# Two up-down filters and an attention block on one core: rows of maxima copied by ACT's transfers, a finer second group norm, the second half's bias on VectorE, and new orders on four engines

## The chip, the core and the metric

One core of a Trainium2 chip runs the whole program. The time is the device time of one execution in microseconds. Engines: PE is TensorE, ACT is ScalarE, DVE is VectorE, POOL is GpSimd; SP is used for issuing transfers only. Each engine works through its own list in order and meets the others through semaphores.

## What is computed

The input x has 8 images of 128 channels and 16 x 16 points. First a filtered leaky ReLU: add a bias per channel, upsample by 2 in both directions with a 12-tap filter, leaky ReLU, downsample by 2 with the same filter. Then, on the result y:

```python
x_norm = group_norm(y, gn1_gamma, gn1_beta, 32)
q, k, v = split(qkv_w @ x_norm + qkv_b)            # 8 heads of 16
attn = softmax(q @ k.T / sqrt(16)) @ v
x_attn = group_norm(out_w @ attn + out_b, gn2_gamma, gn2_beta, 32)
h1, gate = split(x_attn.T @ mlp1_w.T)              # 512 each
out = y + (silu(h1) * gate @ mlp2_w.T).T
```

All tensors are float32.

## The kernel before

The tokens of an image are its 256 points. PE does every filter and every projection; a product marked float32r is one pass, plain float32 costs several.

**Filters.** The input comes as six overlapping windows of rows (`win`), each in two quarters of two images (`in_xw`) and one half of four images (`in_xh`), by 18 transfers that SP issues first. The bias is added in place: for the quarters by DVE (`add_bias`, L1499), for the second half by POOL (`add_bias(t)`, L364, one add of 128x512 per window). `upsample(n)` (L790, n = 0 to 15) multiplies windows with a Kronecker weight into one of four PSUM banks, which `leaky(n)` (ACT, L507) reads out; so `upsample(n)` waits for `leaky(n - 4)`. `downsample(b)` (L822) makes image b, and `read_y(b)` (ACT, L515 and L517) copies it and sums its values and squares.

**First group norm.** `group_means(n)` (PE, L806) averages over groups for one batch of images, `variance(n)` (DVE) follows, `first_coefficients(n)` (POOL, L378 to L381) gives scale and shift. `normalise_first` (DVE) normalises image 0, `normalise(i)` (POOL) the others, each split into a high and a low part.

**Attention, image by image.** `project_qk(i)` and `project_v(i)` go into the bank `px`. `high_parts(i)` (ACT, L524) and `low_parts(i)` (DVE, L1531) write the two parts of q and k to `qk_parts`, and six transfers of SP (`stack(i)`, L311) lay them out as `q_stack` and `k_stack` of 128 rows in one of three slots; `fill` (ACT, L500, 128x2048, six in all) clears the slots once. `maxima(i, h, c)` (L862) is half of the scores of head h in bank `pm[h % 2]`, `reduce_max(i, h)` (DVE, L1548) takes the negative row maximum, and after eight heads `turn_maxima(i)` (PE, L876) turns them into a row layout, which `read_rows(i)` (ACT, L578) copies to `max_row`. The transfer `rows(i)` (SP, L317, 8 KB) puts them into the last row of `q_stack`, so that `scores(i, h, c)` (L888) come out with the maximum subtracted, in bank `ps[h % 2]`. `exponentials(i, h)` (ACT, L531) reads that bank; `scores` of head h waits for the exponential of head h - 2. `weigh(i, half, c)` (L913) multiplies with V and a column of ones. Then for the division: `read_sums` (ACT, L549, L550), `merge` (DVE), `turn_sums` (PE, L924), `invert` (DVE), `spread_inverse` (ACT, L557), `turn_inverse` (PE, L931), `normalise` (DVE, L1575), `project_out` (PE, L936), `read_proj` and `square_attn` (ACT, L566, L572).

**Second group norm and MLP.** `GN2_BATCHES` says for which images one `group_means` and one `second_coefficients` (POOL, seven small steps, L388 to L394) serve. `second_norm(i)` (POOL, L447, L449, L452) writes the high and low part of image i. An image has two pairs p = 2i and 2i + 1. `up_project(p, j, e)` (L772 to L774, three products) makes values (j = 0) and gates (j = 1). For p below 8 ACT's `squash` is a tanh and DVE's `swish_value` and `gate` finish; from p = 8 on `squash` is a Silu, with a table load before the first. `split_high(p)` (ACT, L586) and `split_low(p)` (POOL, L424) split the product for `down_project(p, e)`, up to p = 13; 14 and 15 go in plain float32 (L998). `split_high(p)` waits for `down_project(p - 2)`, `gate(p)` for `split_low(p - 2)`. `residual(i)` (DVE, L1602) adds y, `store(i)` (SP) sends the image out.

**Orders.** For each engine a list is written out by hand at the end of its block; `up_project(14)` and `(15)` belong to image 7. SP's list mixes `stack`, `rows`, `load_w1` and `store`.

Of the kernel before, what the change touches and what calls it, by code (L numbers as in the profile page):

```python
# [31 lines left out]
F32 = mybir.dt.float32  # L32
F32R = mybir.dt.float32r
ALU = mybir.AluOpType
# [41 lines left out]
GN2_BATCHES = [(0, 2), (2, 4), (4, 6), (6, 7), (7, 8)]  # L76
# [4 lines left out]
def build(nc, xw, xh, factors, vecs, wqk, wv, wo, w1, w2,  # L81
          ident, gmat, swap, out):
    ctx = ExitStack()
    with ctx:
# [131 lines left out]
        biased_dve, biased_pool = sem("biased_dve"), sem("biased_pool")  # L216
# [65 lines left out]
        def _(sp):  # L282
# [42 lines left out]
            stack(1)  # L325
            load_w1()
            stack(2)
            rows(0)
            rows(1)
            stack(3)  # L330
            rows(2)
            stack(4)
            rows(3)
            stack(5)
            stack(6)
            rows(4)
            rows(5)
            stack(7)
            rows(6)
            store(0)  # L340
            store(1)
            rows(7)
            for j in range(2, 8):
                store(j)
# [4 lines left out]
        def _(pool):  # L349
# [9 lines left out]

            def add_bias(t):  # L360
                pool.wait_ge(fac_in, 16)
                pool.wait_ge(win_in[t][2], 16)
                x4 = win_at(t, 2, 2).rearrange("p (b c) -> p b c", c=C)
                pool.tensor_tensor(x4, x4, bias_bc[:, None, :].to_broadcast([128, B // 2, C]), ALU.add).then_inc(biased_pool, 1)  # L364
# [90 lines left out]
            for j in range(0, 5):  # L455
                add_bias(j)
# [3 lines left out]
            add_bias(5)  # L460
# [9 lines left out]
            second_norm(0)  # L470
            second_norm(1)
            split_low(0)
            second_coefficients(4)
            second_norm(2)
            second_norm(3)
            for j in range(1, 4):
                split_low(j)
            second_coefficients(5)
            second_norm(4)
            split_low(4)  # L480
            split_low(5)
            second_norm(5)
            split_low(6)
            second_coefficients(6)
# [10 lines left out]
        def _(act):  # L495
# [118 lines left out]
            for j in range(7, 10):  # L614
                leaky(j)
# [1194 lines left out]
```

## Time and profile before

| what | us |
|---|---|
| median of 3 runs | 147.03 (146.26 to 147.64) |
| the profiled execution's own time | 146.93 |
| its span, from the first to the last instruction | 145.1 |
| PE busy / ACT busy / DVE busy / POOL busy | 138.5 / 104.5 / 88.2 / 75.2 |

The profiled execution lies 1.8 us around its span and 0.1 from the median. Busy times are sums over an engine's instructions; matmul ends are modelled. "Idle before, releaser" is the time in which the engine stood still before an instruction, and what released it.

### The profile page before, as it was taken

The page shows a single profiled execution, that of the slowest core. Times are in us where ns is not written, and L with a number is a line of the kernel's source. Part 1 is how long each engine was busy: PE and PEld are TensorE (multiplying, and loading weights), DVE is VectorE, ACT ScalarE, POOL GpSimd, SP SyncE. Part 2 cuts the span into 40 slices and gives each one's busy share as a digit, 9 for nine tenths or more (in the row PEclk, how much of TensorE's full clock was granted, in tenths as well). Part 3 has the DMA queues.
Part 4 walks back from the last instruction along what each step waited for, and adds up shares of the span by engine and source line. Part 5 has one row for each costly group of instructions (what it writes and reads, how often), then busy time and mean ns, then how long its engine had stood idle before and what let it go on. Part 6 is the DMA issues. An engine that isn't in the chain of part 4 may idle for free.

```text
span 145.1 us, 3307 instructions
## 1 busy us (share of the span) xinstructions
PE 138.5 (95%) x1150; PEld 122.2 (84%) x1150; DVE 88.2 (61%) x187; ACT 104.5 (72%) x235; POOL 75.2 (52%) x126
## 2 busy tenths in 40 slices
PE   6999888999999999999999999999999999999992
PEld 5899578999988687788896998797997997999891
DVE  1940133077649679699699889768684715634251
ACT  6956997955448688697793996894995995766330
POOL 7008985066584850402840304892108988589930
PEclk9999999999999999999999999999999999999999
DMA  3999200746530061331606103501001010011012
GB/s 110 285 272 338 91 0 15 205 113 185 178 113 0 10 169 49 106 113 42 182 0 175 53 0 85 138 0 38 0 7 38 0 43 0 0 41 36 0 36 72
DMA packets 12368, 12.12 MB, mean 83 GB/s; under 512 B 1600, under 2 KB 11328, under 8 KB 12352
## 3 DMA queue, kind: packets, MB, share of 16 engines
q1 hardware_dynamic: 12208, 11.81, 27.4%
q8 instruction: 9, 0.15, 0.4%
q10 hardware_dynamic: 144, 0.10, 0.2%
q14 instruction: 7, 0.06, 0.1%
HBM read 4.50 MB, written 1.05 MB: 38 GB/s over the span
## 4 chain that ended last, share of the span: by engine, by line
PE 63%; SPq 10%; POOL 9%; DMA 7%; issue 4%; DVE 3%; POOLq 1%; ACT 1%; ACTq 0%
PE ps L888 10%; PE po L913 10%; PE pm L862 9%; SPq L311 6%; SPq L286 4%; DMA win<-in_xh 4%; PE pf L772 3%; PE pf L774 3%; PE pf L773 3%; PE px L772 3%; POOL gated_lo L424 3%; PE po L936 3%; PE px L774 2%; PE px L773 2%; POOL win L364 2%
## 5 line engine op out<-in xcount | busy, mean ns | idle before, releaser
L1548 DVE TENSOR_REDUCE neg_max<-pm 128x2 f32<-128x512 f32 x64 | 42.3, 683 | 11.8 <-PE pm L862 11.2
L531 ACT ACTIVATE up_t<-ps 128x512 f32<-128x512 f32 x64 | 36.0, 595 | 4.6 <-PE ps L888 2.5
L888 PE MATMUL ps<-q_stack,k_stack 128*128 128x256 f32 x128 | 27.6, 302 | 0.0
L862 PE MATMUL pm<-k_stack,q_stack 127*128 127x256 f32 x128 | 26.3, 300 | 0.3 <-DVE neg_max L1548 0.2
L424 POOL TENSOR_TENSOR gated_lo<-win,gated_hi 128x512 fp32r<-128x512 f32 x14 | 18.1, 1304 | 12.6 <-ACT gated_hi L586 12.6
L888 PEld LDWEIGHTS ps<-q_stack,k_stack 128*128 128x128 f32 x128 | 19.5, 189 | 2.3 <-ACT up_t L531 1.0
L862 PEld LDWEIGHTS pm<-k_stack,q_stack 127*128 127x128 f32 x128 | 19.1, 189 | 2.5 <-DVE neg_max L1548 1.0
L913 PE MATMUL po<-up_t,v_aug 128*32 128x256 f32 x256 | 15.7, 382 | 0.0
L772 PE MATMUL pf<-xm_hi,w_hi 128*128 128x256 f32 x44 | 13.4, 304 | 0.3 <-issue 0.3
L586 ACT ACTIVATE gated_hi<-win 128x512 fp32r<-128x512 f32 x14 | 8.8, 631 | 6.6 <-DVE win L1597 4.4
L773 PE MATMUL pf<-xm_lo,w_hi 128*128 128x256 f32 x44 | 12.3, 280 | 0.0
L774 PE MATMUL pf<-xm_hi,w_lo 128*128 128x256 f32 x44 | 12.3, 279 | 0.0
L388 POOL TENSOR_TENSOR sq<-gs 128x2 f32<-128x2 f32 (+1 forms) x5 | 1.0, 195 | 21.2 <-DVE gs L1505 21.2
L913 PEld LDWEIGHTS po<-up_t,v_aug 128*32 128x32 f32 x256 | 7.6, 109 | 5.0 <-issue 0.2
L364 POOL TENSOR_TENSOR win<-win,fac 128x512 f32<-128x512 f32 x6 | 7.5, 1275 | 8.3 <-DMA win<-in_xh 8.3
L772 PEld LDWEIGHTS pf<-xm_hi,w_hi 128*128 128x128 f32 x44 | 8.3, 189 | 1.3 <-issue 1.3
L790 PE MATMUL pf<-win,up_w 128*128 128x256 f32 x32 | 8.1, 386 | 0.9 <-ACT up_t L507 0.9
L1531 DVE SCALAR_TENSOR_TENSOR qk_parts<-px,vec,qk_parts 128x256 fp32r<-128x256 f32 x16 | 6.9, 470 | 2.9 <-ACT qk_parts L525 2.9
L549 ACT ACTIVATE early<-po,vec 128x256 f32<-128x256 f32 x8 | 3.8, 474 | 6.6 <-PE po L913 6.6
L773 PEld LDWEIGHTS pf<-xm_lo,w_hi 128*128 128x128 f32 x44 | 8.3, 189 | 0.0
L790 PE MATMUL ps<-win,up_w 128*128 128x256 f32 x32 | 8.3, 400 | 0.0
L774 PEld LDWEIGHTS pf<-xm_hi,w_lo 128*128 128x128 f32 x44 | 8.3, 188 | 0.0
(149 smaller groups left out, 344.6 us busy)
## 6 DMA issues: line engine op xcount, KB each, us to landing
q_stack<-qk_parts SPq DMA_DIRECT2D x24, 128.0 KB, 2.4
k_stack<-qk_parts SPq DMA_DIRECT2D x24, 128.0 KB, 2.4
win<-in_xw SPq DMA_DIRECT2D x12, 128.0 KB, 3.2
win<-in_xh SPq DMA_DIRECT2D x6, 256.0 KB, 5.5
out<-win SPq DMA_DIRECT2D x8, 128.0 KB, 1.7
win<-in_w SPq DMA_DIRECT2D x1, 512.0 KB, 3.7
w_s<-in_w SPq DMA_DIRECT2D x1, 256.0 KB, 3.6
wqk_s<-in_wqk SPq DMA_DIRECT2D x1, 128.0 KB, 4.1
```

The source lines that it names most:

```text
L364: pool.tensor_tensor(x4, x4, bias_bc[:, None, :].to_broadcast([128, B // 2, C]), ALU.add).then_inc(biased_pool, 1)
L424: pool.tensor_tensor(gated_lo[:, r, :], gated[:, r, :], gated_hi[:, r, :].bitcast(F32), ALU.subtract).then_inc(gated_split, 1)
L531: act.activation(probs[:, h // HALF, h % HALF, :, :].rearrange("p c n -> p (c n)"), ps[:, h % 2, :], ACT.Exp, scale=D ** -0.5).then_inc(pr ...
L586: act.activation(gated_hi[:, r, :], gated[:, r, :], ACT.Copy).then_inc(gated_hi_ready, 1)
L772: pe.matmul(dst, w_hi, x_hi, start=start, stop=False)
L773: pe.matmul(dst, w_hi, x_lo, start=False, stop=False)
L774: return pe.matmul(dst, w_lo, x_hi, start=False, stop=stop)
L790: mm = pe.matmul(up_bank[n % 4][:, j * Q:(j + 1) * Q], up_w[:, UP_WEIGHT_OF[m], :, :].rearrange("p a b -> p (a b)"), win_at(t, q), start=T ...
L862: return pe.matmul(pm[:, h % 2, c * N:(c + 1) * N], stack_rows(q_stack, i, slice(0, TOP))[:, h, c * 128:(c + 1) * 128], stack_rows(k_stack ...
L888: return pe.matmul(ps[:, h % 2, c * N:(c + 1) * N], stack_rows(k_stack, i, slice(0, TOP + 1))[:, h, c * 128:(c + 1) * 128], stack_rows(q_s ...
L913: mm = pe.matmul(po[32 * g:32 * g + 32, 0, half * N:(half + 1) * N], v_aug[:, i % V_RING, c, half, b + 32 * g:b + 32 * g + 32], probs[:, h ...
L1548: dve.tensor_reduce(neg_max[:, i % 2, 2 * h:2 * h + 2], pm[:, h % 2, :].rearrange("p (c n) -> p c n", c=2), AX.X, ALU.max, negate=True).th ...
```

## The change

1. `rows(i)` leaves SP. `read_rows(i)` on ACT now waits for the stack of image i too, copies, waits for its own copy and issues the same transfer itself. SP's list is `stack(0)`, `load_w1`, `stack(1)` to `stack(7)`, then all stores.
2. The second group norm has six batches, with images 0 and 1 apart.
3. POOL's `add_bias` goes. DVE's `add_bias(t, 2)` does it, 128x512 each, after its other adds.
4. New orders on POOL, ACT, PE and DVE. The cut diff shows their two ends; between them MLP steps come earlier: `up_project(0, 0, 0)` now stands in the `scores` of image 2 (before: of image 3), and at the last `weigh` 10 pairs are up-projected and 8 down-projected (before: 8 and 6).

```diff
-GN2_BATCHES = [(0, 2), (2, 4), (4, 6), (6, 7), (7, 8)]
+GN2_BATCHES = [(0, 1), (1, 2), (2, 4), (4, 6), (6, 7), (7, 8)]
...
-            def rows(i):
-
-                sp.wait_ge(rows_read, i + 1)
-                sp.dma_start(stack_rows(q_stack, i, slice(TOP, TOP + 1)).rearrange("o h (c n) -> o (h c) n", c=2).bitcast(F32),
-                             max_row[:, :].bitcast(F32)).then_inc(row_in, 16)
...
             stack(0)
-            stack(1)
             load_w1()
...
+            for j in range(1, 8):
+                stack(j)
+            for j in range(0, 8):
                 store(j)
...
-                pool.tensor_tensor(x4, x4, bias_bc[:, None, :].to_broadcast([128, B // 2, C]), ALU.add).then_inc(biased_pool, 1)
...
+            split_w1()
             split_w2()
-            split_w1()
...
+            second_coefficients(7)
             second_norm(6)
-            for j in range(7, 10):
+            for j in range(8, 11):
                 split_low(j)
-            second_coefficients(7)
-            split_low(10)
+            second_coefficients(8)
             second_norm(7)
             for j in range(11, 14):
                 split_low(j)
...
             def read_rows(i):
+
+                act.wait_ge(stack_in[i % SLOTS], 32 * STACKED * (i // SLOTS + 1))
                 act.wait_ge(turn_done, i + 1)
                 if i:
                     act.wait_ge(row_in, 16 * i)
                 act.activation(max_row[:, :], pm[0:2 * HEADS, 1, 0:128], ACT.Copy).then_inc(rows_read, 1)
+                act.wait_ge(rows_read, i + 1)
+                act.dma_start(stack_rows(q_stack, i, slice(TOP, TOP + 1)).rearrange("o h (c n) -> o (h c) n", c=2).bitcast(F32),
+                              max_row[:, :].bitcast(F32)).then_inc(row_in, 16)
...
             fill(1, 0)
+            for j in range(6, 10):
+                leaky(j)
             fill(1, 1)
-            leaky(6)
+            read_y(2)
             fill(2, 0)
-            for j in range(7, 10):
+            high_parts(0)
+            for j in range(10, 13):
                 leaky(j)
-            read_y(2)
-            high_parts(0)
-            leaky(10)
+            read_y(3)
+            leaky(13)
+            leaky(14)
             fill(2, 1)
-            read_y(3)
+            leaky(15)
             read_early_v(0)
...
             squash(8)
             squash(9)
-            spread_inverse(7)
+            read_sums(7)
             split_high(8)
             split_high(9)
+            squash(10)
+            squash(11)
+            spread_inverse(7)
+            split_high(10)
             read_proj(7)
-            squash(10)
             square_attn(7)
...
             group_means(0)
-            for j in range(8, 11):
+            upsample(8)
+            upsample(9)
+            downsample(2)
+            downsample(3)
+            project_qk(0)
+            for j in range(10, 15):
                 upsample(j)
-            downsample(2)
-            project_qk(0)
-            downsample(3)
-            upsample(11)
             project_v(0)
...
             weigh(7, 1, 1)
...
             up_project(11, 0, 0)
-            down_project(9, 0)
-            down_project(9, 1)
             up_project(11, 0, 1)
+            turn_sums(7)
             up_project(11, 1, 0)
             up_project(11, 1, 1)
             up_project(12, 0, 0)
+            turn_inverse(7)
+            down_project(8, 0)
+            down_project(8, 1)
+            project_out(7)
+            down_project(9, 0)
+            down_project(9, 1)
             up_project(12, 0, 1)
             up_project(12, 1, 0)
+            group_means(8)
             up_project(12, 1, 1)
             up_project(13, 0, 0)
             up_project(13, 0, 1)
+            up_project(13, 1, 0)
+            up_project(13, 1, 1)
             down_project(10, 0)
             down_project(10, 1)
-            up_project(13, 1, 0)
-            up_project(13, 1, 1)
             up_project(14, 0, 0)
             up_project(14, 0, 1)
             up_project(14, 1, 0)
-            up_project(14, 1, 1)
             down_project(11, 0)
             down_project(11, 1)
+            up_project(14, 1, 1)
...
             def add_bias(t, q):
+                n = 1 if q < 2 else 2
                 dve.wait_ge(win_in[t][q], 16)
-                x4 = win_at(t, q).rearrange("p (b c) -> p b c", c=C)
-                dve.tensor_tensor(x4, x4, bias_bc[:, None, :].to_broadcast([128, B // QUARTERS, C]), ALU.add).then_inc(biased_dve, 1)
+                x4 = win_at(t, q, n).rearrange("p (b c) -> p b c", c=C)
+                dve.tensor_tensor(x4, x4, bias_bc[:, None, :].to_broadcast([128, n * B // QUARTERS, C]), ALU.add).then_inc(biased_dve, 1)
...
             variance(0)
             normalise_first()
             low_parts(0)
             variance(1)
+            for j in range(0, 3):
+                reduce_max(0, j)
             low_parts(1)
-            for j in range(0, 6):
+            for j in range(3, 8):
                 reduce_max(0, j)
```

## Rows read from the trace of the kernel before

**Rows 1.** The page, parts 1 and 2: busy us (share) xinstructions; PE's clock by slices

```profile
PE 138.5 (95%) x1150; PEld 122.2 (84%) x1150; DVE 88.2 (61%) x187; ACT 104.5 (72%) x235; POOL 75.2 (52%) x126
...
PEclk9999999999999999999999999999999999999999
```

**Rows 2.** One stretch, first `scores` to last `weigh`: busy us (instructions), clock, DMA

```profile
core 0: us, PE busy (x) PEld busy (x) DVE busy (x) ACT busy (x) POOL busy (x), PEclk, DMA share, GB/s
42.86:119.50 76.64, 75.94 (x698) 65.22 (x698) 59.35 (x119) 61.15 (x147) 35.04 (x65) 1.00 0.21 59
```

**Rows 3.** The chain that ended last: start us, us, what

```profile
75.25 0.43 PE po L936 x2
...
76.50 0.57 PE px L844 x4
...
117.94 0.12 PE pf L772
...
119.62 1.86 PE po L913 x32
...
124.16 0.22 PE po L924 x2
...
129.00 0.30 PE po L806 x2
...
129.63 0.20 POOL sq L388
...
132.04 1.27 POOL gated_lo L424
...
134.48 0.74 POOL xm_lo L452
...
142.58 0.42 DVE win L1602
```

**Rows 4.** Timeline of the start, all engines: start us, us, engine line op tiles [idle <-releaser]

```profile
6.37 3.11 SPq L286 DMA_DIRECT2D win<-in_xh  x6
...
11.49 6.19 POOL L364 TENSOR_TENSOR win<-win,fac 128x512 f32<-128x512 f32 x5 [8.29 <-DMA win<-in_xh]
...
15.77 0.16 DVE L1514 TENSOR_SCALAR gs<-po 128x2 f32<-128x2 f32 x1 [4.59 <-PE po L806]
...
16.04 1.90 ACT L500 ACTIVATE k_stack<-rest 128x2048 fp32r<-128x2048 f32 x1
...
17.64 0.42 POOL L355 TENSOR_SCALAR wqk_hi<-wqk_s 128x256 fp32r<-128x256 f32 x1
...
18.48 1.13 PE L790 MATMUL pf<-win,up_w 128*128 128x256 f32 x4 [0.92 <-ACT up_t L507]
...
22.27 0.36 PE L772 MATMUL px<-xn_hi,wqk_hi 128*128 128x256 f32 x1 [0.83 <-DVE xn_lo L1526]
```

**Rows 5.** Groups of instructions by line: shapes xcount, busy us, mean ns, idle before us

```profile
L1548 DVE TENSOR_REDUCE neg_max<-pm 128x2 f32<-128x512 f32 x64 | 42.3, 683 | 11.8 <-PE pm L862 11.2
...
L1593 DVE TENSOR_TENSOR win<-win,ps 128x512 f32<-128x512 f32 x2 | 1.4, 688 | 3.8 <-POOL gated_lo L424 2.5 <-ACT win L600 1.3
```

**Rows 6.** The tile `max_row`: its transfers, from issue to landing

```profile
DMA to landing us min/median/max: 1.8/1.8/2.2
```

**Rows 7.** Timeline around the first row transfer

```profile
39.84 0.25 ACT L578 ACTIVATE max_row<-pm 16x128 fp32r<-16x128 f32 x1
...
40.56 0.60 SPq L317 DMA_DIRECT2D q_stack<-max_row  x1
```

**Rows 8.** Who waited for whom, all engines: us in total, times, longest us

```profile
PEld pm L862 <- DMA k_stack<-qk_parts: 0.3, 1, 0.3
```

**Rows 9.** Timeline of the end

```profile
122.72 1.28 ACT L600 ACT_TABLE_LOAD   x1
...
124.02 0.60 ACT L600 ACTIVATE win<-pf 128x512 f32<-128x512 f32 x1
...
135.32 0.36 PE L772 MATMUL pf<-xm_hi,w_hi 128*128 128x256 f32 x1 [0.26 <-issue]
```

More of the change, by code:

```diff
@@ L669, in _ @@
-            exponentials(2, 7)
-            read_sums(2)
+            squash(0)
+            high_parts(6)
             exponentials(3, 0)
             exponentials(3, 1)
-            high_parts(6)
+            read_sums(2)
+            split_high(0)
             exponentials(3, 2)
@@ L1095, in _ @@
             maxima(2, 2, 1)
-            project_v(3)
-            weigh(0, 1, 0)
-            weigh(0, 1, 1)
+            project_qk(4)
             maxima(2, 3, 0)
             maxima(2, 3, 1)
+            turn_sums(0)
             maxima(2, 4, 0)
             maxima(2, 4, 1)
+            turn_inverse(0)
+            maxima(2, 5, 0)
+            maxima(2, 5, 1)
             scores(1, 0, 0)
@@ L1126, in _ @@
             turn_maxima(2)
+            group_means(3)
+            project_qk(5)
             scores(1, 6, 0)
-            project_out(0)
             scores(1, 6, 1)
-            project_v(4)
+            scores(1, 7, 0)
             maxima(3, 1, 0)
@@ L1134, in _ @@
             maxima(3, 2, 1)
-            scores(1, 7, 0)
             scores(1, 7, 1)
@@ L1143, in _ @@
             maxima(3, 4, 0)
+            maxima(3, 4, 1)
             scores(2, 0, 0)
@@ L1147, in _ @@
             scores(2, 1, 1)
-            maxima(3, 4, 1)
-            project_qk(5)
-            scores(2, 2, 0)
+            weigh(1, 1, 0)
+            weigh(1, 1, 1)
             maxima(3, 5, 0)
             maxima(3, 5, 1)
-            turn_sums(1)
+            project_v(5)
+            maxima(3, 6, 0)
+            maxima(3, 6, 1)
+            scores(2, 2, 0)
             scores(2, 2, 1)
             scores(2, 3, 0)
-            scores(2, 3, 1)
-            maxima(3, 6, 0)
-            maxima(3, 6, 1)
-            turn_inverse(1)
             maxima(3, 7, 0)
             maxima(3, 7, 1)
+            scores(2, 3, 1)
+            up_project(0, 0, 0)
+            turn_sums(1)
             scores(2, 4, 0)
             scores(2, 4, 1)
+            up_project(0, 0, 1)
             maxima(4, 0, 0)
@@ L1222, in _ @@
             maxima(5, 2, 1)
-            project_v(6)
-            up_project(0, 1, 0)
+            scores(3, 7, 0)
+            scores(3, 7, 1)
+            up_project(1, 1, 1)
+            project_qk(7)
             maxima(5, 3, 0)
+            scores(4, 0, 0)
+            scores(4, 0, 1)
+            scores(4, 1, 0)
+            scores(4, 1, 1)
             maxima(5, 3, 1)
-            up_project(0, 1, 1)
+            maxima(5, 4, 0)
+            maxima(5, 4, 1)
             weigh(3, 0, 0)
@@ L1635, in _ @@
-            for j in range(5, 8):
+            for j in range(3, 7):
                 reduce_max(1, j)
             low_parts(3)
-            for j in range(0, 4):
-                reduce_max(2, j)
+            reduce_max(1, 7)
+            reduce_max(2, 0)
+            reduce_max(2, 1)
             merge(0)
+            reduce_max(2, 2)
+            invert(0)
+            reduce_max(2, 3)
             reduce_max(2, 4)
+            normalise(0)
             reduce_max(2, 5)
-            invert(0)
+            low_parts(4)
```

665 lines of the change are left out of this document (308 added, 357 removed).

## The prediction, made before the changed kernel was run

> **What bounds the kernel now.** I read the page's busy table and clock row first, then sums over stretches, then the timelines of both ends. The reader is to see in the first that TensorE (PE) is busy 95% of the span at the full granted clock, and ACT, the next, 72% [rows 1]. So the time is PE's work plus the places where PE waits. From the first `scores` to the last `weigh` ACT is busy 61.15 us of 76.64, 80% [rows 2].
>
> I count PE's work by the hand-written order, with starts that follow each other in the trace. One 256-column product of the split projections takes 0.12 us, so a step of three 0.36 and a half of a `maxima` or `scores` 0.12. One image's `weigh` takes 1.86 (with a further 0.2 until the next product, 2.06), `project_v` 0.57, `project_out` 0.43, a turn 0.22, a group mean 0.3 with its wait [rows 3]; without it I take 0.22. From the first `scores` (42.86) to the last `weigh` (119.55) the old order has 128 + 105 halves, 32 up and 12 down steps, 5 `project_qk`, 5 `project_v`, 7 of each turn and of `weigh`: 72.4 us of work in 76.7, so 4.3 us of waits. After the last `weigh` (end W = 121.5) come 19.9 us of work in 21.1, then 2.5 us to the end (the last residual starts at 142.58 [rows 3]; store, landing): the span ends at W + 23.6.
>
> Two large holes stand in the start: PE is idle 0.92 us at 18.48, until ACT, held by a `fill` of 1.90, reads a bank, and 0.83 us at 22.27, until POOL has done its biases and image 0 is normalised [rows 4].
>
> **The start.** POOL's six bias adds of some 1.2 (five in 6.19, from 11.49) go; six on DVE cost 0.69 each, the price of a DVE tensor-tensor of the same 128x512 [rows 5], 4.1 us. Their cover is that DVE stands idle 4.59 us before 15.77, and the landings space them: POOL's first add waits for the first until 11.49, the six issues take 3.11 in all [rows 4], so the last lands at 14 to 14.8, and its add ends by 15.5, before the group mean can be read at 15.77. Without that cover `variance(0)` would slip by up to 0.7. POOL can then split wqk at about 15.8 (its data, issued behind the windows, has to land) instead of 17.64; from there to `project_qk(0)` at 22.27 it was 4.6 us through coefficients and `normalise_first` [rows 4], so the operand is there at 20.4. PE meanwhile does upsample 8, 9 and downsample 2, 3, as ACT now reads banks 6 to 9 before the next fill: work without a hole to 20.9. Both holes go: -0.9 - 0.8, and about 0.4 of slow restarts.
>
> What is late next (the steps between: an activation of 512 columns 0.6 [rows 9], one of 256 some 0.4 to 0.5, `low_parts` 0.87, a hop between engines 0.1, estimates from the same timelines): the fills still cost 1.9 each and now stand later. `fill(2,1)` runs 27.1 to 29.0, then `leaky(15)`, then `read_early_v(0)` to 30.0, and `project_qk(1)` waits for that copy: +0.5. Then DVE paces: `reduce_max` of 0.68 [rows 5] with `low_parts(1)` before the fourth, the eighth ends at 38.8, after `read_y(7)`. Row 0 is read at about 39.4; its transfer of 1.8 us from issue to landing [rows 6] issued at 39.8 lands at 41.6, and the fourth `maxima` of image 1 goes then too: +0.4. First `scores` at 41.65 instead of 42.86: **-1.2**. The bounds are 0 (DVE's chain is as late as before) and -2.1 (nothing late next).
>
> **The row transfers.** Eight issues leave SP and go to ACT. Before, row 0 was copied at 39.84 to 40.09 and issued at 40.56, behind the stack transfers, in 0.60 [rows 7]; the 0.5 of queueing goes, and is in the 41.65. Each issue holds ACT 0.6 or a little less (SP's row, the nearest), and some 0.05 for the wait on its own copy; queued behind it are the next exponential and so the next-but-one `scores`, as `ps` has two banks. Seven in the middle: 7 x 0.65 = 4.5 us on ACT, plus 2 squashes of 0.6 and one copy of V that come before the last `weigh`: 61.2 + 6.1 = 67.3 of about 81. I take 0 on the path: ACT's idle 15.4 us shrinks to about 14. The bounds are -0.5 (rows land earlier) and +4.5 (each issue felt by PE in full).
>
> PE waits once for a stack, 0.3 us, for the k rows of image 3 [rows 8]. Its slot comes free with the last `scores` of image 0, which the new order has ahead of the second half of `weigh(0)` and 1.2 earlier, while the `maxima` that need it come later: **-0.3**.
>
> The Trainium skill ("DMA: Bandwidth & Descriptors", section "Issuing engines are not separate DMA queues") says that initiating DMAs from several engines saves only the sequencer's time to initiate. By that rule the landing stays 1.8 and the one gain is the 0.5 us of queueing, as the row of row 0 has it; were it false, and two queues also landed faster, the sum would be lower by some tenths.
>
> **Batches and orders.** Six batches instead of five add a group mean on PE (0.22) and, on POOL, coefficients of 2.4 us (129.63 to 132.04) [rows 3], beside PE's work: cost 0.2, which is in the start's sum already. What they allow: image 0's MLP starts at 53.5 instead of 61.0 us of PE's priced work, and by the last `weigh` 40 up and 16 down steps are done, not 32 and 12: 8 x 0.355 + 4 x 0.355 = 4.26 more. So the middle is 77.1 us of work, **+4.7** (one `project_v` and less by one `maxima` half beside), and the end 15.7, less by 4.3. If all else stood, that would be a shift of work and nothing else. But the end hangs on a chain, not on work.
>
> **The chain behind the last `weigh`.** Before, read off [rows 3, 9]: group mean at W + 7.5 (129.0), the coefficients to 132.04, one `split_low` of 1.27, the norm of image 7 to 134.48 + 0.74 = 135.2, so 1.9; `up_project(14)` at 135.32 after an idle 0.26, then 7.3 us to 142.58. The old order has 5.7 us of PE work between group mean and `up_project(14)`; so it nearly covers POOL.
>
> After: read sums at W + 0.3; they now come behind the table load of 1.28 and two squashes, which PE's 3.1 us from the last `scores` to W cover. Merge to W + 2.1; `turn_sums`, reciprocal to 3.0; ACT spreads it only behind `split_high(8)`, `(9)`, `squash(10)`, `(11)`: to 3.95; `turn_inverse` 4.0; `down(8)`; `normalise` 4.4 to 4.85; `project_out` 4.95 to 5.4; `split_high(10)` waits for `down(8)` and holds `read_proj` until 5.8; square to 6.95; group mean at W + 7.15. POOL: 0.6 + 2.4 + 1.9, norm done at W + 12.0. On PE only `up(12,1,1)`, `up(13)` and `down(10)` lie between, 0.36 + 1.42 + 0.71 = 2.5 us, from W + 7.4 to 9.9: **a hole of 2.2 us**. Then `up(14)` at W + 12.1 and 7.3 us, of which 0.2 is a wait for `split_low(11)`: W + 19.4, and 2.5: the span ends at **W + 21.9**, where work alone would give W + 18.2. Against the 23.6 of before: -1.7, for 4.3 us of work less. The bounds are -3.5 (W + 20.1: ACT's order costs nothing and every step follows at once) and -0.7 (POOL or ACT late by another 1 us).
>
> The Trainium skill ("ScalarE: Activation LUTs", section "What ACT_TABLE_LOAD costs") gives a load about 1283 ns plus a drain of about 1380. The load here starts at 122.72, takes 1.28, and the next activation starts at 124.02 [rows 9]: no drain behind it. By the page the sums would be read some 1.3 us later.
>
> **The sum**, against the profiled run: -1.2 - 0.3 + 4.7 - 1.7 = +1.5, a span of 146.6 instead of 145.1. With the 1.83 us around the span (146.93 less 145.1) **148.4 us**. The median before, 147.03, is 0.1 above that run. About 1% (1.5 us) is what a measurement of this kernel tells from no change.
>
> **The rivals.**
> A, faster: the middle loses its waits. For it: 4.3 us of them are there, 2.3 of them by 61 us, and more MLP steps lie beside attention from image 0 on, to fill them. Against it: most of them come before the first MLP step. If it loses 3.5 of 4.3, 148.4 - 3.2 = 145.2. It decides for a gain of 1% from 2.9 us on.
> B, slower: ACT becomes the bound of the middle. Its place is the pair of `ps` banks: an issue of 0.65 beside a row copy of 0.25 is longer than the 0.6 by which one exponential leads. For it: ACT at 83% in the middle with exponentials, squashes and splits in one queue; with 3 us of the 4.5 felt, 151.4. It decides from 0.1 us on for 1%.
> C, the end is shorter: ACT's and DVE's steps of the chain come 1.8 us sooner, W + 20.1: 146.6. Against it: the POOL steps, 4.9 us, are read off and can't shrink.
> D, the change doesn't do what it says: the holes of the start return elsewhere and the end is work-bound as before: 147.0.
> E, the drain of the table load, a mechanism of the end: ACT's queue stays shut after the load for as long again as the load of 1.28 [rows 9], before the sums: 149.7. Against it: the 0.02 us behind the load of before.
> The page "ScalarE: Activation LUTs" of the Trainium skill is what speaks for E.
>
> **How the numbers follow.** Forecast 0.38, A 0.22, B 0.20, C 0.10, D 0.08, E 0.02. The forecast's own spread of about 1 us puts 0.24 of its 0.38 within 1% (145.5 to 148.5) and 0.14 above. A gives 0.17 faster and 0.05 same; B 0.19 slower, 0.01 same; C 0.03 faster, 0.07 same; D 0.07 same, 0.01 faster; E slower. In sum faster 0.21, same 0.44, slower 0.35. The range leaves out 1 in 10 on either side: 145.0 (rival A's time, less 0.2) and 150.4 (two thirds of B's 3 us felt).
>
> **What would show it.** Right: PE without a hole over 0.3 us from 15.6 to 27; first `scores` at 41.3 to 42.0; last `weigh` starting at 122 to 123.5; PE idle 1.5 to 3 us before `up_project(14)`, released by POOL's norm; end at W + 21 to 22.5; transfers of rows landing 1.7 to 2.3 after an ACT issue of 0.4 to 0.65. Wrong: the last `weigh` before 121.5 (A), after 125 with PE waiting for ACT's exponentials (B), no hole before `up_project(14)` (C or D).

## The result, and the profile after

The kernel after takes 149.4 us (median of 6, 148.34 to 150.25), the kernel before beside it 146.75 (6 runs): a ratio of 1.019, 95% interval 1.015 to 1.023. It is slower by nearly two per cent. The sum had forecast a loss of a little over half that size, and its 148.4 us is 1.0 short; of the three outcomes, no change had the highest chance. Medians are of all runs; ratios leave out slow runs, over 1.5% above the fastest of the same kernel.

The profiled execution took 150.02 us, 148.2 of them the span. Parts 1 and 2 of the page of the kernel after, as in [rows 1]:

```profile
PE 139.7 (94%) x1152; PEld 123.7 (83%) x1152; DVE 91.5 (62%) x194; ACT 104.1 (70%) x235; POOL 69.3 (47%) x127
...
PEclk9999999999999999999999999999999999999599
```

PE has two products more (the sixth batch) and 1.2 us more of busy time, in a span that is 3.1 longer (products at a lower clock count as longer busy, so the difference in work is not read from here); the clock row, all nines before, dips once, near the end. A view of stretches says where the time went (columns as in [rows 2]: us, busy us of each engine, granted clock, DMA share, GB/s; cut at the first `scores`, the start of the last `weigh`, and the hole behind it):

```profile
15.00:20.00 5.00, 4.53 (x32) 4.17 (x32) 2.18 (x8) 4.55 (x6) 3.37 (x8) 1.00 0.17 58
20.00:25.00 5.00, 5.00 (x33) 4.65 (x32) 1.39 (x3) 4.74 (x11) 1.02 (x2) 1.00 0.08 21
...
41.64:123.54 81.90, 80.51 (x739) 69.67 (x737) 61.03 (x123) 62.35 (x149) 36.93 (x72) 1.00 0.23 65
...
132.00:137.16 5.16, 2.92 (x25) 2.74 (x24) 0.85 (x2) 2.07 (x4) 3.97 (x12) 1.00 0.07 25
137.16:148.20 11.04, 8.46 (x50) 7.90 (x50) 3.34 (x6) 1.83 (x3) 3.71 (x3) 0.83 0.10 36
```

The holes of the start [rows 4] are gone: behind the 0.47 us at its edge in which the group mean waits for its matrix, PE is busy without a break from 15.6 to 25. The first `scores` stands at 41.64; from there to the last `weigh` it is 81.9 us instead of 76.7 [rows 2], where the prediction's prices give 4.7 us more of PE work. In the last two rows PE is idle for 2.24 of 5.16 us, and then the granted clock is 0.83 on average.

The first row transfer in the timeline, against [rows 7]: ACT copies, issues at once, and its next instruction names the copy as what it waited for.

```profile
39.15 0.27 ACT L550 ACTIVATE max_row<-pm 16x128 fp32r<-16x128 f32 x1
...
39.45 0.60 ACTq L552 DMA_DIRECT2D q_stack<-max_row  x1
...
40.16 0.26 ACT L513 ACTIVATE out_bias<-po,vec 128x1 f32<-128x1 f32 x1 [0.74 <-ACT max_row L550]
```

The timeline of the end, against [rows 9]. POOL's chain from the group mean's variance to the norm of image 7 is unbroken, and ends at 137.06; `up_project(14)`, which needs that norm, starts at 137.16 after 2.24 us without a product. From 137.7 to 141.1 one product is followed by the next after 0.21 us, not 0.12:

```profile
131.98 0.35 PE L779 MATMUL po<-mv,gmat_s 128*128 128x2 f32 x2
...
132.67 0.19 POOL L361 TENSOR_TENSOR sq<-gs 128x1 f32<-128x1 f32 x1 [0.46 <-DVE gs L1478]
...
134.64 0.28 PE L750 MATMUL px<-gated_hi,w_lo 128*128 128x256 f32 x1
...
136.34 0.72 POOL L425 TENSOR_TENSOR xm_lo<-up_t,xm_hi 128x256 fp32r<-128x256 f32 x1
...
137.16 0.36 PE L748 MATMUL pf<-xm_hi,w_hi 128*128 128x256 f32 x1 [2.24 <-issue]
...
138.16 0.42 PE L748 MATMUL pf<-xm_hi,w_hi 128*128 128x256 f32 x1
...
138.37 0.42 PE L749 MATMUL pf<-xm_lo,w_hi 128*128 128x256 f32 x1
...
138.58 0.42 PE L750 MATMUL pf<-xm_hi,w_lo 128*128 128x256 f32 x1
```

The end in both kernels and in five of the experiments below, read off their timelines (us; "behind" is from the end of the last `weigh` to the end of the span; the work beside it is what PE's order holds behind the last `weigh`, by the prices of the prediction):

| profiled run | last `weigh` ends | last group mean | `up_project(14)` | span ends | behind | PE work behind |
|---|---|---|---|---|---|---|
| before | 121.5 | 129.0 | 135.3 | 145.1 | 23.6 | 19.9 |
| after | 125.5 | 132.0 | 137.2 | 148.2 | 22.7 | 15.7 |
| e3, hole filled | 125.4 | 132.0 | 137.2 | 146.9 | 21.4 | 15.7 |
| e10, new middle and end | 126.4 | 133.0 | 138.2 | 147.8 | 21.4 | 15.7 |
| e2, old end | 123.8 | 131.2 | 137.6 | 147.4 | 23.6 | 19.9 |
| e11, half held | 124.1 | 131.2 | 137.5 | 147.3 | 23.2 | 17.8 |
| e12, six batches | 123.1 | 130.7 | 136.9 | 146.8 | 23.6 | 19.9 |

### The profile page after: what moved, and what is told of

The parts are those of the page before. It is cut to its first block, busy times and chain, and to the rows that moved or that the text cites. A ratio compares the mean times of both kernels' runs of the same rounds, so it can differ in the third digit from the quotient of the medians.

```text
span 148.2 us, 3318 instructions
## 1 busy us (share of the span) xinstructions
PE 139.7 (94%) x1152; PEld 123.7 (83%) x1152; DVE 91.5 (62%) x194; ACT 104.1 (70%) x235; POOL 69.3 (47%) x127
## 4 chain that ended last, share of the span: by engine, by line
PE 80%; SPq 6%; DMA 5%; DVE 3%; issue 3%; ACT 1%; ACTq 0%
PE ps L861 11%; PE po L886 10%; PE pm L835 10%; SPq L286 5%; PE pf L748 4%; PE pf L749 4%; PE pf L750 4%; PE px L748 3%; DMA gmat_s<-in_gmat 3%; PE px L749 3%; PE px L750 3%; PE px L817 3%; PE ps L763 2%; PE pf L763 2%; PE pm L795 2%
## 5 line engine op out<-in xcount | busy, mean ns | idle before, releaser
L501 ACT ACTIVATE up_t<-ps 128x512 f32<-128x512 f32 x64 | 35.2, 599 | 9.2 <-PE ps L861 5.6
L835 PE MATMUL pm<-k_stack,q_stack 127*128 127x256 f32 x128 | 27.7, 306 | 0.6 <-DVE neg_max L1521 0.5
L861 PE MATMUL ps<-q_stack,k_stack 128*128 128x256 f32 x128 | 25.5, 296 | 0.3 <-DMA q_stack<-max_row 0.3
L861 PEld LDWEIGHTS ps<-q_stack,k_stack 128*128 128x128 f32 x128 | 18.8, 189 | 2.4 <-issue 0.8
L749 PE MATMUL pf<-xm_lo,w_hi 128*128 128x256 f32 x44 | 12.8, 290 | 0.0
L1472 DVE TENSOR_TENSOR win<-win,fac 128x256 f32<-128x256 f32 (+1 forms) x18 | 8.9, 513 | 2.5 <-DMA win<-in_xw 2.1
L378 POOL TENSOR_SCALAR win<-y,scale,shift 128x256 f32<-128x256 f32 x7 | 4.0, 576 | 9.0 <-PE px L817 8.7
L748 PE MATMUL px<-gated_hi,w_hi 128*128 128x256 f32 x24 | 7.8, 325 | 0.0
```

The costliest lines, as they stand in the source:

```text
L501: act.activation(probs[:, h // HALF, h % HALF, :, :].rearrange("p c n -> p (c n)"), ps[:, h % 2, :], ACT.Exp, scale=D ** -0.5).then_inc(pr ...
L748: pe.matmul(dst, w_hi, x_hi, start=start, stop=False)
L749: pe.matmul(dst, w_hi, x_lo, start=False, stop=False)
L835: return pe.matmul(pm[:, h % 2, c * N:(c + 1) * N], stack_rows(q_stack, i, slice(0, TOP))[:, h, c * 128:(c + 1) * 128], stack_rows(k_stack ...
L861: return pe.matmul(ps[:, h % 2, c * N:(c + 1) * N], stack_rows(k_stack, i, slice(0, TOP + 1))[:, h, c * 128:(c + 1) * 128], stack_rows(q_s ...
L1472: dve.tensor_tensor(x4, x4, bias_bc[:, None, :].to_broadcast([128, n * B // QUARTERS, C]), ALU.add).then_inc(biased_dve, 1)
```

## The experiments

Twelve kernels ran. The kernel before ran beside each group (medians of 146.6 to 147.2 us); times are medians, ratios are to it.

**Parts alone.** First the start by itself: the second half's bias goes to DVE, and PE's, ACT's and DVE's orders are those of the kernel after up to the first scores, then the rest of the kernel before's.

```
-                    if q < 2:
-                        pe.wait_ge(biased_dve, NWIN * q + t + 1)
-                    else:
-                        pe.wait_ge(biased_pool, t + 1)
+                    pe.wait_ge(biased_dve, NWIN * min(q, 2) + t + 1)
...
             stack(0)
-            stack(1)
             load_w1()
+            stack(1)
             stack(2)
             rows(0)
```

> The kernel before with the new start alone: bias of the second half on DVE, the new orders of all engines up to the first scores, then the old orders; rows by SP, five batches. Theory (the loss of the change comes behind the last weigh, the new start is a gain of 1.2 us of which the attention's first waits may take some back): 1.2 us faster than before, ratio 0.992; at least not slower than 0.998. Rival 1 (the new start is late for DVE and ACT, and its gain is lost at once): ratio 1.000. Rival 2 (the bias on DVE is part of the loss): over 1.005.

152.31 us, ratio 1.041 (1.032 to 1.050): by the number the second rival, but not for its reason. SP's issues and the first `scores` in its timeline:

```profile
38.58 0.27 ACT L578 ACTIVATE max_row<-pm 16x128 fp32r<-16x128 f32 x1
...
43.55 0.61 SPq L311 DMA_DIRECT2D k_stack<-qk_parts  x1
...
44.21 0.60 SPq L317 DMA_DIRECT2D q_stack<-max_row  x1
...
46.17 0.58 PE L898 MATMUL ps<-q_stack,k_stack 128*128 128x256 f32 x1 [2.72 <-DMA q_stack<-max_row]
```

The row was copied at 38.58 and issued at 44.21: `rows(0)` stands behind `stack(2)` on SP, and the new orders make that stack's parts later and the row earlier. So the run shows nothing of the start; it shows that the start needs the row out of the stacks' way, on ACT or ahead of `stack(2)`. The run with that one line moved:

```
             stack(1)
-            stack(2)
             rows(0)
+            stack(2)
```

> As the earlier run with the new start alone on the kernel before (second half's bias on DVE, new orders up to the first scores, rows issued by SP, five batches), with one thing changed: on SP the first row transfer stands ahead of the third stack, not behind it. Left of the whole change: its start. Theory (the 5.6 us lost there were the row waiting behind that stack's issues): row issued at 38.6 to 39.6, first scores at 41.2 to 41.9, accumulation in the middle as in the kernel before, 145.2 to 146.0 us. Rival (the new start itself delays DVE or ACT, and the row only hid it): first scores at 41.2 to 41.9 all the same, but the gain is gone by scores(1,0), 146.5 to 147.5. Second rival (something else than the row held the first scores): first scores after 44, over 150.

147.33 us, ratio 1.004 (1.000 to 1.008). The 5 us came from that place, but not from the wait alone: the profiled spans differ by 3.9 us, 2.7 of them the wait. The rest is the clock behind it: with the wait, the granted clock was 0.50 from 44 to 48 and six products of `project_qk` followed each other after 0.21 us, not 0.12. The time of this run is the first rival's, but the first `scores` came at 43.44, later than either theory has it, because the joined order had left `project_v(2)` ahead of it, where PE waited 0.97 us. With it behind, as in the kernel after:

```
-            project_v(2)
             scores(0, 0, 0)
             scores(0, 0, 1)
+            scores(0, 1, 0)
+            scores(0, 1, 1)
+            maxima(1, 4, 0)
+            maxima(1, 4, 1)
+            project_v(2)
```

> As the run with row 0 first (the kernel before with the new start alone, rows by SP, row 0 ahead of the third stack), with one thing changed: project_v(2) and ACT's copy of its result stand behind the first four scores, as in the kernel after; in both earlier runs of this start they stood ahead of them, and PE waited 0.97 us there for the low parts on DVE and spent 0.43 us on the projection. Left of the whole change: its start. Theory (the whole of what the start lost there is this wait): first scores at 41.4 to 42.0, accumulated work and waits 1.0 to 1.5 us under that run to the end, 145.8 to 146.4 us, a ratio to the kernel before of 0.992 to 0.998. Rival (DVE's or ACT's queue behind the start gives the gain back in the first head pair): first scores at 41.4 to 42.0 and 146.6 to 147.4 us.

147.38 us, ratio 1.005 (1.001 to 1.009), 12 runs. The rival holds. The first `scores` is at 41.49, 1.4 earlier than in the kernel before, and `scores(1, 0, 0)` is at 51.86, where it was at 51.92. PE's waits in the window 40 to 46 of its timeline:

```profile
41.15 0.50 PE L872 MATMUL pm<-k_stack,q_stack 127*128 127x256 f32 x2 [0.55 <-DVE neg_max L1564]
...
42.62 0.68 PE L854 MATMUL px<-wv_s,win 128*128 128x128 f32 x4 [0.26 <-DVE qk_parts L1547]
...
43.87 0.36 PE L785 MATMUL px<-xn_hi,wqk_hi 128*128 128x256 f32 x1 [0.56 <-ACT v_aug L537]
```

The wait at 41.15 is ahead of the first `scores`. Behind it stand 0.26 and 0.56, for DVE's low parts and for ACT's copy of V; a further 0.19 at 45.96 is in the kernel before too. Another 0.57 of the 1.4 was never a gain: it is `project_v(2)`, which stands ahead of the first `scores` in the kernel before and behind it here. `project_qk(3)` starts at 43.87, where it was at 43.94, so the gain has gone 2.4 us after the first `scores`.

The complement, the new middle and end (six batches, the kernel after's orders from the first scores on) behind the old start, rows by SP:

```
-GN2_BATCHES = [(0, 2), (2, 4), (4, 6), (6, 7), (7, 8)]
+GN2_BATCHES = [(0, 1), (1, 2), (2, 4), (4, 6), (6, 7), (7, 8)]
```

> The complement of the run with row 0 first: the kernel before's start (bias on POOL, its orders up to the first scores) and rows by SP in the kernel before's SP order, with six batches and the kernel after's orders from the first scores to the end. First scores at 42.6 to 43.0. If the parts add, it is the kernel after less ACT's issues plus the start's gain given up: 149.4 - 2.2 + 1.1 = 148.3 (147.9 to 148.8). If the new middle and end cost nothing by themselves and only ACT's issues did, 146.7 to 147.3; if they cost all of it and ACT's issues nothing, 150 to 151.

157.72 us, for the first experiment's reason, at another place (and again with the clock at 0.50 behind the wait, from 85 to 91); SP's queue and PE in its timeline:

```profile
77.69 0.25 ACT L587 ACTIVATE max_row<-pm 16x128 fp32r<-16x128 f32 x1
...
83.50 0.60 SPq L317 DMA_DIRECT2D q_stack<-max_row  x1
...
85.48 0.79 PE L910 MATMUL ps<-q_stack,k_stack 128*128 128x256 f32 x2 [4.93 <-DMA q_stack<-max_row]
```

Row 4 stood behind `stack(6)`, which the new orders make later. With `rows(4)` ahead of `stack(6)` and `rows(0)` ahead of `stack(2)`:

> As the earlier run of the new middle and end behind the old start (six batches, orders of the kernel after from the first scores on, rows by SP), with SP's order mended: row 4 stands ahead of the seventh stack, row 0 ahead of the third. In the earlier run row 4 was copied at 77.9 and issued at 83.5, and PE stood idle for 4.9 us before scores(4,0). Theory (that wait and what it pushed is all that was wrong, and the parts add): first scores at 42.6 to 43.3, no idle over 0.5 before scores(4,0), last weigh starts at 124 to 125, 149.4 to 150.4 us, which is the kernel after plus the start's 1.1 with nothing back for ACT's issues. Rival (rows by SP give the 2 us back that ACT's issues cost in the old orders): 147.4 to 148.4 us.

150.03 us, ratio 1.023 (1.018 to 1.028). So the new middle and end cost over 2% by themselves (2.8 us by medians of all runs, some 3.4 by the ratio). With the new start before them the ratio is 1.019; the intervals overlap, but the timelines tell the start's worth. The first `scores` is at 42.88 here and at 41.64 in the kernel after, the first `weigh` at 46.56 and 45.83, the last at 124.52 and 123.54. Of the 1.2 us, 0.57 is again `project_v(2)`, now behind the first `scores`; the other 0.7 arrives and stays. In the old orders nothing of it did. (PE still waited 0.45 us before `scores(4, 0, 0)`, for a row that took 3.0 us to land.)

Six batches alone; the added group mean stands ahead of `weigh(1)`:

> The kernel before with six batches in the second group norm and nothing else: windows 0 and 1 get a batch each; the one more group mean stands ahead of weigh(1), its reading behind reduce_max(3,2), the coefficients of window 0 and its second norm on POOL one batch early; all other steps in the kernel before's order. Theory (the batches are free where they stand, the cost of the change is in the end): one product pair of some 0.2 us more on PE, one more short chain on DVE and POOL, 146.8 to 147.4 us against 146.9, a ratio of 0.999 to 1.004. Rival (the group mean waits on ACT's squares in front of weigh(1) and holds the attention behind it): 0.6 us and more, over 147.5.

148.14 us, ratio 1.008 (1.005 to 1.011). The rival holds. Two lines of PE in its timeline:

```profile
58.96 0.35 PE L815 MATMUL po<-mv,gmat_s 128*128 128x2 f32 x2 [0.36 <-ACT y_squares L581]
...
59.76 0.59 PE L922 MATMUL po<-up_t,v_aug 128*32 128x256 f32 x5 [0.45 <-DVE gs L1520]
```

The first `scores` is 0.1 us earlier than in the kernel before, and the last `weigh` starts 1.6 us later. The products of the group mean take 0.2 us, but PE waits 0.36 for ACT's squares ahead of them and 0.45 behind them, because `weigh` writes the bank from which DVE still has to read the means. That is about 1.0 us, the price at this place; of a wait of 0.42 us for k rows, at 55.9, the kernel before had 0.3 [rows 8]. In the kernel after the group mean stands elsewhere, and its price there was not measured alone.

**Who issues the rows.** The kernel before, with the row transfers alone moved to ACT (`read_rows` waits for the image's stack too, as in the kernel after; ACT never stood idle there in this trace):

```
                 act.activation(max_row[:, :], pm[0:2 * HEADS, 1, 0:128], ACT.Copy).then_inc(rows_read, 1)
+                act.wait_ge(rows_read, i + 1)
+                act.dma_start(stack_rows(q_stack, i, slice(TOP, TOP + 1)).rearrange("o h (c n) -> o (h c) n", c=2).bitcast(F32),
+                              max_row[:, :].bitcast(F32)).then_inc(row_in, 16)
```

> The kernel before with the rows' transfers issued by ACT alone, every order else as before. Theory (an issue of 0.5 to 0.6 on ACT hides in ACT's idle time): within 0.5 us of before, ratio 0.998 to 1.004. Rival B of the prediction (ACT is the bound of the middle): 7 issues felt in half or more, 2 us or more, ratio from 1.014. A second rival: rows that land earlier gain, ratio under 0.998.

149.09 us, ratio 1.017 (1.011 to 1.023): 2.5 us slower. Its profiled span is 1.7 longer, and three waits of PE behind such issues hold 1.06 of it in plain idle time (0.21, 0.60, 0.25); the second and the third of them in its timeline:

```profile
66.49 0.25 ACT L569 ACTIVATE max_row<-pm 16x128 fp32r<-16x128 f32 x1
...
66.77 0.51 ACTq L571 DMA_DIRECT2D q_stack<-max_row  x1
...
67.38 0.42 ACT L562 ACTIVATE y_squares<-up_t 128x256 f32<-128x256 f32 x1 [0.64 <-ACT max_row L569]
...
68.04 0.35 PE L800 MATMUL po<-mv,gmat_s 128*128 128x4 f32 x2 [0.60 <-ACT y_squares L562]
...
87.62 0.53 ACTq L571 DMA_DIRECT2D q_stack<-max_row  x1
...
88.25 0.60 ACT L521 ACTIVATE up_t<-ps 128x512 f32<-128x512 f32 x1 [0.66 <-ACT max_row L569]
...
88.90 0.38 PE L882 MATMUL ps<-q_stack,k_stack 128*128 128x256 f32 x1 [0.25 <-ACT up_t L521]
```

An issue shut ACT's compute for 0.64 to 0.66 us. Where the group mean's squares were queued next, PE waited 0.60 of it; where it was an exponential, 0.25. The other way round, the kernel after with the rows back on SP, each ahead of the stack two further on:

> The kernel after with one thing taken back: SP issues the eight row transfers, each ahead of the stack two further on (rows 0 ahead of stack 2, and so on), and ACT no longer waits for the stack before its copy. Theory A (ACT's issues are what the middle paid for: they cost the kernel before 2.5 us when ACT took them over): PE's accumulated waits at scores(7,7) fall from 5.1 to 2.5 to 3.5 us, last weigh starts at 121.0 to 122.0, 147.0 to 147.8 us. Theory B (the middle pays for its own work and its order, ACT's issues lie beside): the waits stay within 0.5 us and the time at 149.0 to 149.8. First scores stay at 41.3 to 42.0 in both.

149.74 us, ratio 1.017 (1.008 to 1.026): theory B. Beside the 1.019 of the kernel after, ACT's issues cost nothing in the new orders that can be measured. That speaks against theory A (147.0 to 147.8), but with four runs some tenths of a microsecond would not be seen, and SP's own queueing is in the number. (In its profiled execution the last k rows of one stack took 4.2 us to land, and PE waited 0.6 us; in that of the next run they took 2.3.)

**The end.** The kernel after with 17 products that nobody reads in the hole, writing a bank that is free there:

```
+            def keep_busy(n):
+                pe.wait_ge(gn_read, len(GN_BATCHES))
+                for _ in range(n):
+                    pe.matmul(po[:, 0, 0:N], w1_hi[:, 0:C], w1_hi[:, 0:N], start=True, stop=True)
...
             down_project(10, 1)
+            keep_busy(17)
             up_project(14, 0, 0)
```

> The changed kernel with 17 products of 0.12 us in the hole before up_project(14), which write a bank that is overwritten later (they add nothing to the output). Theory of two parts (2.2 us of waiting for POOL, and behind it some 3.4 us at the lower clock, 16 products of 0.21 instead of 0.12): the hole's time stays, the lower clock goes, so 1.0 to 1.5 us less than the changed kernel in runs where that showed the lower clock, ratio to before 1.008 to 1.012. Rival (the lower clock has nothing to do with the hole): the same low stretch and the same time, ratio 1.016 to 1.02.

148.68 us (148.59 to 148.99), ratio 1.014 (1.009 to 1.018), 0.7 below the kernel after by medians. The two intervals overlap (1.015 to 1.023 there), so the size is not well known. The stretches in it that answer to the last two of the kernel after:

```profile
132.00:137.15 5.15, 4.90 (x41) 4.73 (x41) 0.84 (x2) 2.02 (x4) 3.96 (x12) 1.00 0.07 25
137.15:146.90 9.75, 7.12 (x50) 6.45 (x50) 3.27 (x6) 1.83 (x3) 3.72 (x3) 0.97 0.12 40
```

`up_project(14)` starts at the same 137.15, so the filling makes nothing ready sooner; but the granted clock stays at 0.97, and the last stretch takes 9.75 us instead of 11.04.

The clock of the single executions bears on it. Three kernels have the hole (the kernel after, with rows on SP, and the new middle and end on the old start): six of their 14 executions have a mean clock of 0.987 to 0.989, all others at least 0.998. With the hole filled it is none of eight. But the hole is not the only place: four of the ten executions of the kernel with row 0 first show the same 0.987 or 0.988, without a hole in the end, and so does one of 16 of the kernel before. The profiled run there is at 1.0, so no trace shows where. The same filling with the rows on SP:

> As the run before it (kernel after, rows by SP), with 17 products that nobody reads put behind down_project(10), where PE stands idle for 2.2 us in the kernel after; they write a bank that is free there. If the two costs add, it is 0.6 to 0.8 us below the run before it: 146.3 to 147.1 under theory A, 148.3 to 149.1 under theory B. If the hole changes its size because ACT is early, the filling costs what it saves and the two runs are within 0.3 us.

148.78 us, ratio 1.013 (1.007 to 1.019): within 0.1 of the run with the rows on ACT, theory B a second time.

The kernel after with four MLP steps (`up_project` 8 and 9, `down_project` 6 and 7) taken back behind the last `weigh`, in the kernel before's orders there:

> The changed kernel, but the MLP's advance at the last weigh taken back: up_project 8 and 9 and down_project 6 and 7 stand behind it, and from there on the orders of before. Theory: the span ends 23.6 us behind the last weigh, which comes 4.3 us earlier than in the changed kernel (125.4), so a span of 144.7 and a time 3 us below the changed kernel's, ratio to before 0.995 to 1.00; no hole over 0.5 us and no lower clock in the end. Rival (ACT's issues or the fuller middle cost the time, the end only shifts work): the time of the changed kernel within 0.7 us, ratio 1.014 to 1.02.

149.66 us, ratio 1.020 (1.014 to 1.027): the rival's time. The last `weigh` ends 1.7 us earlier, not 4.3. PE waits beside the last scores for what the steps had covered:

```profile
118.17 0.70 PE L927 MATMUL po<-weighted,wo_s 128*128 128x256 f32 x2 [0.52 <-DVE weighted L1573]
...
120.01 0.50 PE L879 MATMUL ps<-q_stack,k_stack 128*128 128x256 f32 x2 [0.68 <-ACT up_t L507]
```

Half of that, only `up_project(9)` and `down_project(7)` held back:

> The kernel after with half of what the run with the old end took back: only up_project(9) and down_project(7) go behind the last weigh (six products' groups of 0.355, 2.1 us of PE), up_project(8) and down_project(6) stay beside the scores of the last head pair; behind the last weigh the kernel before's orders. Theory (the loss is in the end: advanced steps fill ACT-bound waits beside the last scores, but more than is needed there, and then are missing between group mean and up_project(14)): accumulated work and waits at the last scores 141.1 to 142.2, no idle over 0.5 us before up_project(14), granted clock 1.0 there, the end longer than that sum by 3.7 as in the kernel before: span 144.8 to 145.9, 146.6 to 147.7 us. Rival (ACT's work in the last pair is too late whatever PE has beside it, so the waits of 2.2 us that the full taking back showed return in full): last weigh starts at 122.8 to 123.6, 148.3 to 149.3 us.

149.38 us, ratio 1.019 (1.014 to 1.025). Neither theory. The last `weigh` started at 122.02, 1.5 earlier, there was no hole before `up_project(14)` and no low clock. But two waits stood behind the last `weigh`, which had been covered:

```profile
125.02 1.28 ACT L581 ACT_TABLE_LOAD   x1
...
126.13 0.41 PE L915 MATMUL po<-swap_s,dens 128*128 128x128 f32 x2 [0.77 <-DVE merged L1558]
...
126.32 0.60 ACT L581 ACTIVATE win<-pf 128x512 f32<-128x512 f32 x1
...
127.76 0.44 PE L922 MATMUL po<-ident_s,inv_wide 128*128 128x128 f32 x2 [0.52 <-ACT inv_wide L533]
```

With an earlier last `weigh` the sums are still read, merged and inverted at ACT's and DVE's pace. In the table the group mean moves from 132.0 to 131.2 only, and `up_project(14)` is 0.3 us later, not earlier.

Why so little comes back ahead of the last `weigh` is seen in the stretch from the start of `weigh(6)` to that of `weigh(7)` in the four timelines (us; work by the prices of the prediction):

| profiled run | `weigh(6)` | `weigh(7)` | stretch | PE work in it | up and down steps, counted as in the prediction |
|---|---|---|---|---|---|
| before | 109.94 | 119.55 | 9.61 | 9.3 | 8 / 4 |
| after | 112.08 | 123.54 | 11.46 | 11.5 | 12 / 6 |
| e11, half held | 112.05 | 122.02 | 9.97 | 9.3 | 8 / 4 |
| e2, old end | 112.05 | 121.82 | 9.77 | 7.2 | 4 / 2 |

Everything that the two runs took back came from this stretch, and with less work than some 9.7 us in it PE waits for ACT and DVE instead. The kernel after has four more up and two more down steps than the kernel before ahead of `weigh(6)` as well; no run took those back.

No version beat the kernel before.

## Why the prediction was right in its direction, and where it was short

- **The first `scores`:** 41.65 predicted, 41.64 measured, by the path described: no PE hole between the group mean and 25 us, the row copied at 39.15, issued at 39.45 and landed 1.9 us later.
- **That this -1.2 goes into the sum:** it holds in the new orders. The sum took -1.2 at the first `scores` and put one `project_v` more (0.57) into the middle, so some -0.7 net; the kernel after is 0.73 ahead of the run with the old start at the first `weigh`, and 0.98 at the last. In the old orders the same start gave nothing: PE's next waits, 0.26 and 0.56 us, took it back within 2.4 us. The line "Then DVE paces" was read up to the first `scores` and no further; that the new orders have other work at that place was not part of the argument.
- **The middle:** the first term that was too small. Work +4.7 and stack -0.3 were to make the stretch 4.4 us longer; it became 5.2 longer (81.9 against 76.7), with the last `weigh` at 123.54, just past the upper end of 122 to 123.5. The priced work is 77.1, so the waits grew from 4.3 to 4.8 where the sum had them shrink to 4.0. PE's named waits in the stretch are 1.08 us (0.24 for low parts, 0.38 and 0.20 at `turn_sums(0)` and `turn_inverse(0)`, 0.26 for row 4), against 0.39 before: that is 0.7 of the 0.8. Nothing of rival A was seen.
- **ACT's issues:** the value of 0 on the path held in the new orders within the scatter (ratios 1.017 and 1.013 with SP, 1.019 and 1.014 with ACT). Rival B is refuted for this kernel, but in the old orders the same edit costs 2.5 us, near the 3 that B had given it. The issue took 0.51 to 0.61 us; from issue to landing it was 1.8 to 2.8 us, median 2.1, where the sign to look for had been 1.7 to 2.3.
- **The hole:** 2.2 us predicted, 2.24 measured, at the place named and behind the chain named; the group mean was at W + 6.6 instead of W + 7.15, `up_project(14)` at W + 11.7 instead of W + 12.1. That the size fits to 0.04 is luck in part: PE and POOL were both some 0.5 early.
- **The end:** W + 21.9 predicted, W + 22.7 measured in the profiled run. With the hole filled it is W + 21.4, and W + 21.4 too in the run with the new middle and end on the old start, which has a hole of 2.28 us and kept its clock. So the chain was priced 0.5 too long, and 1.3 was missing altogether: the products behind the hole were priced at 0.12 us, and took 0.21. This is the second term that was too small. It does not strike every execution: two of the six of the kernel after show a mean clock of 0.987 and 0.989 (spans 148.2 and 148.4), the other four at least 0.998 (146.5 to 147.9). By medians the filling gave back 0.7.
- **Rivals C, D and E:** C's shorter end is there in part once the clock is kept (21.4, between 21.9 and 20.1), hidden by the clock in the profiled run. D falls: the start's holes did not return. E falls: in the kernel after the load stands at 123.47 for 1.28 us and the next activation at 124.77, in the half-held run at 125.02 and 126.32, 0.02 behind it both times. The trace goes against the drain that the Trainium skill ("ScalarE: Activation LUTs", section "What ACT_TABLE_LOAD costs") adds to a load.

In spans the forecast was 146.6 and the profiled run 148.2: 0.8 of the difference is the middle, and 0.8 the end (1.3 for the clock, less 0.5). In medians it is 1.0, because that run is one of the two with the low clock. Had the chain not been priced too long, the sum would have been further off.

Of the core of the forecast, two parts are to be kept apart. Between the two kernels it stands: 4.7 us more of work ahead of the last `weigh` made that stretch 5.2 longer, and 4.2 us less behind it made the end 0.9 shorter, or 2.2 with the clock kept, since a chain of waits and not PE's work sets that end. Over the seven rows of the table the work behind the last `weigh` differs by 4.2 us, and the time behind it by 2.2. But that the moved steps are the cause of the loss is not shown: taking them back gave 1.7 us ahead of the last `weigh` and cost 0.9 behind it (2.2 against the runs with the clock kept), and the time stayed. That run and the one with half of it took their steps from the last stretch, where up to some 9.7 us of work costs nothing.

What stays open: whether the kernel gets back to the old time when steps are taken out ahead of `weigh(6)` and not behind it (not tried); what the sixth batch costs at its place in the kernel after, which the middle's 0.8 could contain; whether an order of ACT that reads the last sums and projection ahead of its splits would shorten the chain (not tried); and why the clock falls behind the hole in some executions and not in others, and in some kernels without one.

## What to carry to other kernels

Before you move work ahead of the last step of a dependent chain, measure the chain from that step to the end: if it is longer than the work that lies beside it, the end gets shorter by less than the work that left it. And look at the stretch where the work goes: where the other engines set its length (here some 9.7 us between the last two `weigh`), steps up to that length are free, and taking them out again gives nothing. An issue moved to another engine's queue costs what is queued behind it there, and one left on its queue costs what is ahead of it: the same row transfers on ACT were free in one order and 2.5 us in the other, and on SP one row behind the wrong stack cost 5 us. A gain at the start is read at the next place at which another engine paces, and less the work that was only moved behind the mark; the first instruction that comes sooner does not tell it.

## What the runs showed of the hardware that I had not expected

- Behind 2.24 us without a product, TensorE's products went from 0.12 to 0.21 us apart from 137.7 to 141.1, that is at the lower of its two levels (1.2 instead of 2.4 GHz), and the granted clock of the last stretch was 0.83; with 17 unread products in the hole it was 0.97 and that stretch 1.3 us shorter. In the profiled run with the new middle and end behind the old start a hole of 2.28 us stood, products stayed 0.12 apart and the mean clock was 1.0. In the two kernels with longer waits for a misplaced row (2.72 and 4.93 us in the profiled runs) all eight executions show a lower mean clock (0.976 to 0.977, and 0.966 to 0.988).
- A DMA issue on ACT took 0.51 to 0.61 us, about what one takes on SP, and in the two places shown ACT's next activation began 0.64 and 0.66 us after the end of the copy.
- One 128 KB stack transfer took 4.2 us from issue to landing in one profiled run and 2.3 in the next of nearly the same kernel: a PE wait of 0.6 us in a single trace can be that execution's alone.
